# Ones in the attention key rows set ahead of the sums, eight gathers without an index copy, 22 filler products for 29

## The reference, cut to what matters

```python
x = x + tanh(g_xattn[0]) * L0_xattn(layernorm(x), ctx)      # latent cross attention, 16 items of 128 x 256
x = x + tanh(g_ffn[0])   * L0_ffn(layernorm(x))             # 16 experts, top 2, and one shared
# L1_xattn: 8 heads over the rows, no weights
qk  = einsum('bhdq,bhdl->bhql', qh, kh) * scale             # q from layernorm(x), k = v = ctx
ret = einsum('bhql,bhdl->bhdq', softmax(qk), vh)
x = x + tanh(g_xattn[1]) * gamma * ret
x = x + tanh(g_ffn[1])   * L1_ffn(layernorm(x))             # 8 experts, top 2, three layers
```

## Time and profile before

| | us |
|---|---|
| median of 3 runs | 896.05 |
| lowest, highest | 892.02, 898.84 |
| the profiled execution, its own time | 894.22 |
| its span, first to last instruction | 892.6 |
| mean granted TensorE clock | 0.914 |

### The profile page before, as it was taken

One profiled execution on the slowest core, in us unless ns is written; L12 is line 12 of the kernel. 1 busy time (PEld: TensorE's weight loads), 2 busy tenths in 40 slices (PEclk: granted clock), 3 DMA queues, 4 the chain that ended last, 5 costly groups with the idle time before them and its releaser, 6 DMA issues.

```text
span 892.6 us, 16887 instructions
## 1 busy us (share of the span) xinstructions
PE 732.7 (82%) x4021; PEld 529.9 (59%) x4022; DVE 509.6 (57%) x1349; ACT 328.3 (37%) x857; POOL 350.7 (39%) x363
## 2 busy tenths in 40 slices
PE   4878887878788998999999982399999999999800
PEld 2555665546555645666666651278788888888700
DVE  3638676573233347878888736345555655555533
ACT  1231241212343440555555551145444454545400
POOL 6244444261122253334444223860093548000175
PEclk9658999689899999999999996699999999999965
DMA  8921311053533338877777402551143141110135
GB/s 231 364 92 48 119 47 48 1 188 98 184 114 120 102 93 150 143 125 146 150 152 150 92 26 79 175 188 37 40 131 132 38 129 41 35 41 18 41 113 165
DMA packets 71339, 97.91 MB, mean 110 GB/s; under 512 B 11264, under 2 KB 59744, under 8 KB 71168
## 3 DMA queue, kind: packets, MB, share of 16 engines
q1 hardware_dynamic: 52960, 47.28, 22.0%
q0 software_dynamic: 14944, 47.89, 16.8%
q10 hardware_dynamic: 3392, 2.23, 0.8%
HBM read 63.81 MB, written 33.29 MB: 109 GB/s over the span
## 4 chain that ended last, share of the span: by engine, by line
PE 65%; DVE 10%; issue 7%; POOL 6%; DMA 5%; ACT 3%; ACTq 1%; SPq 1%; POOLq 0%; DVEq 0%
PE ps L1759 23%; PE ps L1696 6%; PE ps L1601 4%; PE ps L1786 4%; PE ps L1641 3%; PE ps L1591 3%; PE ps L1665 3%; PE ps L1611 3%; PE ps L1678 2%; DVE mraw L1053 2%; PE ps L1516 2%; POOL wraw L660 2%; POOL R L666 2%; DMA yg<-Q 2%; PE ps L1477 2%
## 5 line engine op out<-in xcount | busy, mean ns | idle before, releaser
L1759 PE MATMUL ps<-WR,Hap 128*128 x468 | 116.9, 398 | 4.0 <-DVE Hap L1209 4.0
L1358 ACT ACTIVATE Q<-ps 128x512 f32<-128x512 f32 x128 | 75.7, 599 | 68.6 <-PE ps L1678 68.6
L1399 ACT COPY Q<-ps 128x512 f32<-128x512 f32 x78 | 45.8, 587 | 143.7 <-PE ps L1759 143.6
L1053 DVE TENSOR_REDUCE mraw<-ps 128x2 f32<-128x512 f32 x128 | 87.1, 683 | 18.5 <-PE ps L1665 18.3
L1759 PEld LDWEIGHTS ps<-WR,Hap 128*128 128x128 f32 x468 | 85.0, 188 | 21.1 <-issue 4.7
L1696 PE MATMUL ps<-Q 128*32 128x256 f32 x512 | 67.7, 385 | 12.6 <-ACT Q L1358 12.6
L1207 DVE CAST Hbp<-ps 128x512 fp32r<-128x512 f32 x39 | 27.0, 692 | 77.6 <-ACT ps L1393 77.6
L1759 PE MATMUL ps<-WR,Hbp 128*128 x468 | 65.2, 289 | 2.9 <-DVE Hbp L1209 2.9
L1759 PE MATMUL ps<-WR,XTp 128*128 x234 | 62.2, 402 | 1.3 <-DVE XTp L1209 1.3
L1665 PE MATMUL ps<-QK 96*128 96x256 f32 x256 | 58.3, 311 | 4.1 <-DVE mraw L1053 2.6
L327 POOL DMA_DIRECT2D yg<-Q x46 | 25.0, 543 | 91.1 <-ACT Q L1321 91.0
(11 more groups left out here) (263 smaller groups left out, 1545.2 us busy)
## 6 DMA issues: line engine op xcount, KB each, us to landing
Q<-xg SPq DMA_DIRECT2D x86, 128.0 KB, 2.1
QK<-kscr SPq DMA_DIRECT2D x48, 128.0 KB, 3.8
QK<-qscr SPq DMA_DIRECT2D x48, 128.0 KB
yg<-Q POOLq DMA_DIRECT2D x47, 128.0 KB, 2.0
wraw<-in_W POOLq DMA_DIRECT2D x10, 512.0 KB, 8.4
wraw<-in_W POOLq DMA_DIRECT2D x5, 1024.0 KB, 7.6
yg<-Q SPq DMA_DIRECT2D x39, 128.0 KB, 1.7
qscr<-split SPq DMA_DIRECT2D x32, 128.0 KB, 2.4
```

Of the source, the lines that this page charges most:

```text
L1053: v.tensor_reduce(mraw[:, b, h, :], ps[:, h % 2, :].rearrange("p (c l) -> p c l", c=2), AX, ALU.max).then_inc(s["s_max"], 1)
L1358: a.activation(PTb[:, h % 4].rearrange("p c q -> p (c q)"), ps[:, 2 + h % 2, :], ACT.Exp, scale=DH ** -0.5).then_inc(s["st_exp"], 1)
L1399: a.copy(pre, ps[:, bank, :]).then_inc(s[f"l1_h{which}_copied"], 1)
L1759: i = mm(out, parts(x_part, k), ring[:, bass.ds(place, 1), o:o + width].rearrange("p r n -> p (r n)"), start=(k == 0 and x_part == 0 and w ...
```

## The change

In turns -4 to -1 VectorE no longer fills `KS`. Places 0, 1 and 2 are filled by VectorE at the start of stage C, ahead of all its sums, and place 3 by ScalarE, behind its zeros for `QS`. SyncE's waits follow: `q_zeroed` is waited for ahead of the key stack, one count higher for the fourth item. Gathers with a constant item number (items 0 to 7, that is those of the written-out turns) read their indices straight from `yslot`, without copy and wait. The filler ahead of the first scores is 22 products, not 29.

```diff
 def sp_turn(t, k):
...
                     else:
-                        sp.wait_ge(s["phase_done"], t + 5)
+                        sp.wait_ge(s["phase_done"], min(t + 5, NC))
+                        sp.wait_ge(s["q_zeroed"], t + 4 + (t + 3 == NC - 1))
                     alone(sp)
                     stack(KS, kscr, t + 3, n, (0, 1, 0), f"k_stacked{b}")
                     sp.wait_ge(s[f"q_stored{b}"], (t + 3) // 2 * 32 + 32)
-                    if not item(t - 1):
-                        sp.wait_ge(s["q_zeroed"], t + 4)
...
+            N_DIRECT = 8
+
             def gather(items, n, yg, turn, buf, ix, done):
 
+                if isinstance(items, int):
+                    alone(pool)
+                    for k in range(2):
+                        pool.indirect_dma_start(buf[:, k, :], None, yg[:, :],
+                                                bass.IndirectOffsetOnAxis(ap=yslot[:, items, k:k + 1], axis=0)).then_inc(s[done], 16)
+                    return
                 nc.gpsimd.tensor_copy(idxg[:, ix, 0:n], yslot[:, items, :]).then_inc(s["idx_copied"], 1)
-                pool.wait_ge(s["idx_copied"], turn)
+                pool.wait_ge(s["idx_copied"], turn - N_DIRECT)
...
             def c_gather(t, b):
...
-                gather(bass.ds(t, 1), 1, yg0, t + 1, gC[:, b], b, f"gathered{b}")
+                gather(t if isinstance(t, int) else bass.ds(t, 1), 1, yg0, t + 1, gC[:, b], b, f"gathered{b}")
...
             dve.sem_inc(s["phase_done"], 1)
+            for n in range(NC - 1):
+                v.memset(KS[:, n].bitcast(F32), 1.0).then_inc(s["phase_done"], 1)
...
-                if isinstance(t, int) and t < 0:
-
-                    v.memset(KS[:, t + NC].bitcast(F32), 1.0).then_inc(s["phase_done"], 1)
...
                 a.copy(QS[:, n], zeros[:].unsqueeze(1).to_broadcast((P, NH, D))).then_inc(s["q_zeroed"], 1)
+            a.copy(KS[:, NC - 1].rearrange("p a (c q) -> p (a c) q", c=2), ones[:].unsqueeze(1).to_broadcast((P, 2 * NH, P))).then_inc(s["q_zeroed"], 1)
...
-            fill(29, 2 * D)
+            fill(22, 2 * D)
```

## The result

17 runs of each, side by side: the changed kernel 893.0 us median (882.1 to 899.17), the kernel before 895.64 (889.87 to 901.6). The ratio of the two is 0.9949, with a 95% interval of 0.9924 to 0.9974: about 4.6 us less, between 2.3 and 6.8. That ratio is of fast runs alone and leaves out the six of the changed kernel's runs (895.69 to 899.17) that lie over 1.5% above its lowest, 882.1, and none of the kernel before's, which reach 901.6. With all 17 of each the medians are 2.6 us apart, and drawing the 17 times of each anew at random puts the ratio between 0.994 and 1.001. So the gain is a few microseconds, if it is there at all. My forecast was 4.2 less. The size is one that these figures allow. The way to it is not what the trace shows, and most of what follows is about that.

What follows compares the result with a forecast made beforehand. It took the wait chain at the seam of stages B and C as the bound: filler, and a memset between turns -2 and -1. Terms -2.4 - 2.1 - 0.9 + 1.2 = -4.2 us, median 896.05 to 891.9, range 886.5 to 896.7.

Steps and rivals of the forecast that it cites:

- Filler and the query stack's landing: Ahead of stage C's first scores: item 0's stack lands at 338.5, so 22 products start them 2.4 us earlier.
- my own sign of being wrong: In the trace: sums after 326, first score before 337 or after 340, or turn -1 waiting for its stacks.
- My upper bound of 3.2: For the shorter filler: first score 1.6 to 3.2 us earlier, by when item 0's query stack lands.
- Low clock ahead of turn -2: TensorE's 3.5 us idle before the first score lowers its clock in turn -2: +1.2 us, bounds 0 and 2.6.
- Memset between the turns: Between turns -2 and -1 on VectorE: the fourth memset leaves the path, -2.1 us.
- Low clock in turn -1: With the old idle at 349.4 gone, the low clock at 352.7 goes too: -0.9 us, bounds 0 and -1.3.
- rival (c): A later wait, item 1's stacks or the maxima's round trip, catches the gain: -2, 894.0; chance 0.15.
- Direct gathers: Start of stage C: without index copies item 0's sums come 0.3 us earlier, given back on the full DMA system.
- The ones' cover: Before item 0's sums: three memsets hide in the gather wait, ScalarE's fourth fill delays nothing; cost 0.
- Rival (b): Three back-to-back memsets starve the first gather, item 0's sums start 3.4 us later: +0.6, 896.6; chance 0.12.
- (a): TensorE's clock holds through the 3.5 us idle, so the 1.2 is not paid: -5.4, 890.7; chance 0.15.
- (d): Item 0's query stack lands near 336, filler was 5 us too long, no clock loss: -8, 888; chance 0.10.

Runs made afterwards that it cites:

- e1: The kernel before with only the filler cut from 29 to 22 products; ratio to before 0.9986 (0.9964 to 1.0009).
- e7: The changed kernel run again, unedited, on a slower chip; ratio to before 1.0021 (0.9984 to 1.0058).
- e11: The changed kernel, but in turn -2 VectorE does item 2's sums, statistics and query split ahead of item 0's eight maxima; ratio to before 0.9952.
- e12: The same as e11 with 29 filler products instead of 22; ratio to before 0.9937 (0.9914 to 0.9961).
- e3: The kernel before with only the direct gathers (indices from `yslot`), filler 29, memsets as before; ratio to before 0.9995 (0.9974 to 1.0017).
- e2: The kernel before with only the ones moved (three memsets ahead, fourth place by ScalarE, SyncE's waits), filler 29; ratio to before 0.9986.
- e4: The changed kernel with 29 filler products instead of 22; ratio to before 0.9976 (0.9944 to 1.0007).
- e8: The changed kernel with key stacks of items 0 to 3 issued one step earlier, each ahead of its item's query store; ratio to before 1.0004.
- e9: The same as e8 with 25 filler products instead of 22; ratio to before 0.9987 (0.9958 to 1.0015).
- e5: The changed kernel with key stacks of items 0 to 2 issued before the first query store, on a slower chip; ratio to before 1.0008.
- e10: The kernel before run again, unedited; no ratio given, first product with the values 45.2 us behind the first filler.
- e6: The same as e5 with 29 filler products; one run only, no ratio, first product with the values 43.5 us behind the first filler.

## Why the prediction was right or wrong

**Filler and the query stack's landing, forecast -2.4: wrong.** This is the step that failed. By my own sign of being wrong, too: the first score was to come by 340, and with the first filler 1.1 us early in this execution its 340.03 is 341.1 on the clock of the kernel before. I had no row for the landing and took that of key stacks, 5.3 us, for 338.5. e1, with everything else as before, has item 0's stack issued at 17.2 and its first score at 23.7: 6.5 us, above all of the key stacks' 4.8 to 6.0. So only 1.1 to 1.2 us of the filler were waste. My upper bound of 3.2 was also added up wrong: from 338.0 it is 2.95. The changed kernel loses even these: its store of item 0 waits 4.57 us where before 3.59 passed, and its stack is used 6.8 us behind its issue. From item 0's store to the first score it is 11.4 us there, 10.6 in e7, 10.9 and 11.4 in e11 and e12, and 10.1 in e1; how it divides between the store and the stack differs from trace to trace (the store waits 3.9 and 3.6 us in e11 and e12). Gathers and item 1's transfers come earlier in the changed kernel and share the DMA engines, for which I had given back 0.3 us. That they are the cause is likely and not shown: e3 and e2 each move a part of that work without the long store (2.9 and 3.6 us), and their filler hides the rest. Measured for the term: +0.1 (-0.3 in e7).

**Low clock ahead of turn -2, forecast +1.2: right in kind.** The clock was low for some 6.8 us, 2.4 of them in TensorE's idle time; turn -2 took 7.24 us for 6.35, +0.9 (7.37 in e7).

**Memset between the turns, -2.1: right**, 2.06 us became 0.03.

**Low clock in turn -1, -0.9: right in kind, too small.** Turn -1 took 7.07 us for 8.36, -1.3; nothing of the round trip of the maxima showed.

**Later waits: I named the wrong ones.** My rival (c) named item 1's stacks or the maxima's round trip. It was item 2's stacks, whose query is stored behind the maxima of turn -2. Sum at the end of turn -1: +0.1 + 0.9 - 2.1 - 1.3 = -2.4, as the marks show (-2.3); at the first score of turn 0 it is -1.0 and at the values -1.1. So 1.2 us were given back. e2 shows it clean (3.3 gained, 2.9 waited), and e11 and e12 show the cause: with that query stored 4.2 to 5.4 us earlier, and the key stack behind it issued as much earlier, the wait at turn 0 is gone, though a part of it comes back at turn -1. The query stack alone is not the whole of it. From its issue to turn 0's first score, where TensorE waited for it, it is 6.0 to 7.4 us with item 2's key stack issued right ahead of it (the changed kernel, e7, e2, e4), and 5.2 and 5.5 with that key stack issued long before (e8, e9). So the key stack beside it is likely a part of the wait. From the values to the last transposed scores the traces take 175.0 to 175.8 us, and 183.2 to 184.3 on the slower chip (e5 to e7), so what the seam gives reaches the end of stage C.

**The total.** The traces account for 0.6 to 1.1 us. The medians of all 17 runs are 2.6 apart and can't be told from no change; the ratio of 0.9949 says 4.6. e4, which differs only by the seven products, gives 2.1 with an interval that includes none (0.9976), and on the other chip the changed kernel showed no gain at all (1.0021). The profiled execution's own 6.7 us are mostly its luck ahead of the filler (1.1) and behind stage C (4.6), which e7 did not repeat. The order of the ratios follows that of the seams on the other chips (45.0 to 45.5: 0.9986 to 1.0004; e11 and e12, 43.5 and 42.9: 0.9952 and 0.9937), but the 4.3 and 5.6 us of e11 and e12 are over twice the 1.6 and 2.2 of their seams. Why they gave more than the seam stays open. So the forecast of 4.2 agrees with the measured time by luck: its largest term, -2.4, measured +0.1, and a wait that it did not have took back 1.2 of the rest.

**Direct gathers, -0.3 on the first sums: not told from the scatter.** It was 8.85 to 8.61 us in these two traces. But the kernels with copies range over 8.8 to 9.1 (before, e10, e1, e2) and those without over 8.6 to 9.3, e5 and e6 aside. What holds in every trace is the first indirect DMA: 4.46 to 4.50 us behind the first filler without a copy, 4.67 to 4.73 with it, 0.2 and not the 0.4 that I took. The rest of the way to item 0's split query gave it back: the aggregation waits 0.50 us, as in every trace with the memsets ahead, e2 too, and in none with them in the turns. I did not find out for what.

**The ones' cover: right.** ScalarE's fill of the fourth place ran from 323.25 for 1.90 us and nothing waited for it; the three memsets ended ahead of the gather.

**Rival (b), starved gathers: wrong.** GpSimd in the changed kernel, beside the memsets at 319.62 and 321.76:

```profile
319.65 1.02 POOL L550 DMA_INDIRECT gC<-yg,yslot  x1 [2.35 <-DMA yg<-Q]
320.98 0.98 POOL L550 DMA_INDIRECT gC<-yg,yslot  x1 [0.30 <-issue]
322.26 0.95 POOL L550 DMA_INDIRECT gC<-yg,yslot  x1 [0.30 <-issue]
323.51 0.95 POOL L550 DMA_INDIRECT gC<-yg,yslot  x1 [0.30 <-issue]
```

All four take 0.95 to 1.02 us, as elsewhere. A memset by itself does not hold them off, and the rule of the Trainium skill that I weighed against it ("SBUF — State Buffer", "Who interferes with whom": one SBUF input at most and no two-port mode, no contention with GpSimd on trn2) is what this trace shows. The 1.97 us of before were more than a memset alone, but they went with the memsets in the turns: the second DMA of item 2's gather takes 1.97 and 1.98 us in e10 and e1, 2.89 in e3, which keeps the memsets there and drops the copies, and 0.96 in e2, which keeps the copies and moves the memsets. What it is in that place that holds the DMA is not shown.

**Rivals (a) and (d)** did not happen: the clock fell, and no data came early.

## What to carry to other kernels

Filler ahead of a wait says nothing of how long the wait would be: remove some of it alone first and read where the engine then stops, before counting it as a gain. When a pipeline starts up, follow each of its first items to the engine, not only the first: here item 2's query, stored behind the maxima of item 0, became the bound as soon as two microseconds went elsewhere. Where an engine waits at the head of a queue for seven microseconds, move the next items' work in front of that wait: with 29 products that shortened the seam by 1.9 us (e4 to e12), where ones, gathers and filler together gave 1.1. It was tried only with the ones moved, not alone.

## What I had not expected of the hardware

A 128 x 2048 float32 memset has a row of 1.76 us in every case, but back to back they start every 2.14 us: each costs 0.38 us more than its row, which shows as idle in front of it. A stack of three transfers of 128 KB onto 32 partitions each is used 5.2 to 7.4 us behind its issue where TensorE waits for it, 5.5 even in e5 (issued at 348.19, first score 353.67), where no key stack is beside it. And the length of an idle stretch did not settle what the clock did behind it: after 1.48 us of idle in e12 and 1.71 and 1.66 in e9 it stayed at 1.00, but after 1.49 in e7 it fell, as after 1.97 in the kernel before and 2.90 in e2.
